# Six attention layers on one core: the odd heads' softmax exponentials move to ScalarE, head by head out of PSUM

## The reference

```python
q = l2norm(q) * qs ; k = l2norm(k) * ksc
q = q * cos * scale + rotate_half(q) * sin * scale
k = k * cos / scale + rotate_half(k) * sin / scale
sim = einsum('bhwie,bhwje->bhwij', bq, bk2) * 8.0
sim = where(mask, -max, sim)
attn = softmax(sim, -1)
out = einsum('bhwij,bhwje->bhwie', attn, bv2)
```

## Time and profile before

| | |
|---|---|
| median of 3 runs | 1926.08 us (1924.15 to 1927.91) |
| the profiled execution | span 1924.9 us; the page gives no other time of it |
| PE busy | 1751.1 us, 91% of the span |
| PEld busy | 1185.3 us, 62% |
| DVE busy | 1550.0 us, 81% |
| ACT busy | 1138.0 us, 59% |
| POOL busy | 1259.8 us, 65% |
| mean granted TensorE clock | 0.958 of full |
| chain that ended last | PE 40%, DVE 22%, issue 11%, POOL 9%, DMA 7%, ACT 4% |

### The profile page before, as it was taken

How to read it: one execution, slowest core, us unless ns; L and a number is a source line. 1 busy time by engine, 2 the same in 40 slices (tenths; PEclk the granted TensorE clock), 3 DMA queues, 4 the chain that set the end, 5 groups by cost and what they waited for, 6 DMA issues and landing times.

```text
span 1924.9 us, 72907 instructions
## 1 busy us (share of the span) xinstructions
PE 1751.1 (91%) x31158; PEld 1185.3 (62%) x31158; DVE 1550.0 (81%) x2150; ACT 1138.0 (59%) x2221; POOL 1259.8 (65%) x981
## 2 busy tenths in 40 slices
PE   7577876899999989999899999899998999999985
PEld 2144553466666666667666767666666676666663
DVE  6599957788888878888888888788887888888853
ACT  5523223557676747676667676667675667676742
POOL 3476743777777767777667777677776777777730
PEclk9699977999999989999999999999998999999986
DMA  4534201222222232222322222322223222222220
GB/s 97 127 53 51 29 3 70 58 67 70 69 73 68 72 104 79 63 75 70 112 66 79 69 73 83 103 62 77 69 72 109 69 68 79 63 76 67 70 61 26
DMA packets 68257, 137.27 MB, mean 71 GB/s; under 512 B 17952, under 2 KB 23520, under 8 KB 66912
## 3 DMA queue, kind: packets, MB, share of 16 engines
q1 hardware_dynamic: 67936, 132.62, 27.0%
HBM read 29.79 MB, written 2.10 MB: 17 GB/s over the span
## 4 chain that ended last, share of the span: by engine, by line
PE 40%; DVE 22%; issue 11%; POOL 9%; DMA 7%; ACT 4%; SPq 2%; DVEq 0%; ACTq 0%; POOLq 0%
PE bank L1460 9%; PE bank L1370 6%; PE bank L1443 6%; POOL rot L1308 5%; DMA v_shift<-v_tok 5%; DVE rot L1770 5%; PE bank L1418 5%; PE bank L1501 3%; PE bank L1375 3%; PE bank L1477 3%; DVE total L1796 2%; DVE rnorm L1776 2%; POOL probs L1332 2%; DVE probs L1789 2%; DMA p_T<-p_blocks 1%
## 5 line engine op out<-in xcount | busy, mean ns | idle before, releaser
L1770 DVE TENSOR_TENSOR rot<-bank,gains 128x1024 f32<-128x1024 f32 x384 | 462.3, 1206 | 158.8 <-ACT squares L1603 142.8
L1314 POOL TENSOR_TENSOR rot<-rot,rnorm 128x1024 f32<-128x1024 f32 x192 | 361.0, 1901 | 319.3 <-ACT rnorm L1613 317.1
L1308 POOL TENSOR_TENSOR rot<-rot 128x512 f32<-128x512 f32 x384 | 480.6, 1274 | 6.9 <-DVE rot L1770 6.9
L1370 PE MATMUL bank<-wqkv,x 128*128 128x512 f32 x768 | 404.9, 612 | 10.5 <-issue 5.0
L1603 ACT ACTIVATE squares<-bank 128x512 f32<-128x512 f32 x384 | 232.8, 606 | 256.5 <-PE bank L1370 255.9
L1332 POOL TENSOR_TENSOR probs<-probs,total 128x1024 f32<-128x1024 f32 x96 | 182.7, 1903 | 125.3 <-DVE total L1798 125.3
L1644 ACT ACTIVATE o_T<-bank 128x512 f32<-128x512 f32 x192 | 104.2, 598 | 254.2 <-PE bank L1443 254.2
L1776 DVE TENSOR_REDUCE rnorm<-squares 128x16 f32<-128x1024 f32 x192 | 233.0, 1214 | 2.8
L1443 PE MATMUL bank<-p_T,v_shift 64*64 64x32 f32 x6144 | 194.7, 223 | 26.6 <-DMA p_T<-p_blocks 21.9
L1443 PEld LDWEIGHTS bank<-p_T,v_shift 64*64 64x64 f32 x6144 | 169.2, 138 | 79.1 <-issue 49.6
L1383 PEld LDWEIGHTS bank<-st_ident,rot 128*128 128x128 f32 x1536 | 179.9, 143 | 59.9 <-issue 53.6
(11 more groups left out here) (196 smaller groups left out, 2849.2 us busy)
## 6 DMA issues: line engine op xcount, KB each, us to landing
p_T<-p_blocks SPq DMA_DIRECT2D x768, 64.0 KB
v_shift<-v_tok SPq DMA_DIRECT2D x96, 384.0 KB, 3.5
v_shift<-v_tok SPq DMA_DIRECT2D x96, 128.0 KB, 3.4
wqkv<-in_wqkv SPq DMA_DIRECT2D x6, 1536.0 KB, 8.0
v_rep_sb<-v_by_step SPq DMA_DIRECT2D x32, 128.0 KB
v_rep<-v_by_step SPq DMA_DIRECT2D x32, 128.0 KB
wo<-in_wo SPq DMA_DIRECT2D x6, 512.0 KB, 8.6
w<-in_w SPq DMA_DIRECT2D x6, 341.0 KB, 8.8
```

The source lines that it names most:

```text
L1308: nc.gpsimd.tensor_tensor(out=out, in0=out, in1=by_head(turned[:, part])[:, :, frm], op=ALU.add).then_inc(rot_added.sem, 1)
L1314: nc.gpsimd.tensor_tensor(out=by_head(qk[u][:, half]), in0=by_head(qk[u][:, half]), in1=rnorm[u][:, AH * i:AH * (i + 1)].unsqueeze(2).to_b ...
L1370: nc.tensor.matmul(QK_BANKS[i][:, :], shifted_tokens(x, n, P), layer_cols(wqkv, n, 3 * INNER, 512 * i, 512), start=True, stop=True).then_i ...
L1770: nc.vector.tensor_tensor(both, src.unsqueeze(1).to_broadcast([P, 2, 8, DH]), pair_of_gains.unsqueeze(2).to_broadcast([P, 2, 8, DH]), ALU. ...
```

## The change

`shifts` and `totals` handle the even heads only (bank 4). The odd heads' exponentials are taken by ACT straight from bank 5, one head at a time: eight activations of 64 columns, each with the head's negated peak as its per-row bias, and each writing the head's sum as a second result into `total`. The even heads keep one exponential, now over 8 x 64 columns. The factor 8 moves from the activation into the query's rotary tables on the host. `peaks` does the odd heads first, and negates them. `exp_made` counts two per block, the first after the odd heads. PE's wait in `outputs` is now for `shifted` (bank 4 read by DVE) and for `exp_made(.., 1)` (bank 5 read by ACT).

```diff
-    s_product, peak_made, shifted, exp_made = sig("s_product"), sig("peak_made", per=2), sig("shifted", per=2), sig("exp_made")
+    s_product, peak_made, shifted, exp_made = sig("s_product"), sig("peak_made", per=2), sig("shifted"), sig("exp_made", per=2)
...
             else:
+                pe.wait_ge(exp_made.sem, exp_made.after(n - 1, 1))
                 transposes(S_BANKS, q_turned, qk[n % 2][:, 0:INNER], oT_made, n - 2)
...
                 if n < LAST - 1:
                     pe.wait_ge(shifted.sem, shifted.after(n + 1))
+                    pe.wait_ge(exp_made.sem, exp_made.after(n + 1, 1))
...
         def exponent(n):
+            u = n % 2
+            act.wait_ge(peak_made.sem, peak_made.after(n, 1))
+            act.wait_ge(p_turned.sem, p_turned.after(n - 2))
+            act.wait_ge(p_normed.sem, p_normed.after(n - 2))
+            for a_ in range(PAIRS):
+                head = nc.scalar.activation(probs[u][:, a_, 1, :], s_banks(n)[1][:, 2 * WINDOW * a_:2 * WINDOW * (a_ + 1)], ACT.Exp,
+                                            bias=peak[u][:, 1, a_:a_ + 1], accum_out=total[u][:, 2 * a_ + 1:2 * a_ + 2])
+            head.then_inc(exp_made.sem, 1)
             act.wait_ge(shifted.sem, shifted.after(n))
-            pr = probs[n % 2][:, :, :, :].rearrange("p a b d -> p (a b d)")
-            nc.scalar.activation(pr, pr, ACT.Exp, scale=QK_SCALE).then_inc(exp_made.sem, 1)
+            pr = probs[u][:, :, 0, :]
+            nc.scalar.activation(pr, pr, ACT.Exp).then_inc(exp_made.sem, 1)
...
-            for p in range(2):
+            dve.wait_ge(exp_made.sem, exp_made.after(n - 2, 1))
+            for p in (1, 0):
                 s = s_banks(n)[p][:, :].rearrange("p (a k) -> p a k", a=PAIRS)
-                nc.vector.reduce_max(peak[n % 2][:, p, :], s, AX).then_inc(peak_made.sem, 1)
+                nc.vector.tensor_reduce(peak[n % 2][:, p, :], s, AX, ALU.max, negate=(p == 1)).then_inc(peak_made.sem, 1)
...
-            for p in range(2):
-                s = s_banks(n)[p][:, :].rearrange("p (a k) -> p a k", a=PAIRS)
-                dve.wait_ge(peak_made.sem, peak_made.after(n, p + 1))
-                nc.vector.tensor_tensor(probs[n % 2][:, :, p, :], s, peak[n % 2][:, p, :].unsqueeze(2).to_broadcast([P, PAIRS, DH]),
-                                        ALU.subtract).then_inc(shifted.sem, 1)
+            dve.wait_ge(peak_made.sem, peak_made.after(n))
+            s = s_banks(n)[0][:, :].rearrange("p (a k) -> p a k", a=PAIRS)
+            nc.vector.tensor_tensor(probs[n % 2][:, :, 0, :], s, peak[n % 2][:, 0, :].unsqueeze(2).to_broadcast([P, PAIRS, DH]),
+                                    ALU.subtract).then_inc(shifted.sem, 1)
...
-            nc.vector.reduce_sum(total[u][:, :], probs[u][:, :, :, :].rearrange("p a b d -> p (a b) d"), AX).then_inc(total_made.sem, 1)
+            nc.vector.reduce_sum(total[u][:, :].rearrange("p (a b) -> p b a", b=2)[:, 0, :], probs[u][:, :, 0, :], AX).then_inc(total_made.sem, 1)
...
-    for s in (scale, f(1.0) / scale):
+    for s in (f(QK_SCALE) * scale, f(1.0) / scale):
```

More of the change, by code:

```diff
@@ L1432, in outputs @@
                     pe.wait_ge(shifted.sem, shifted.after(n))
+                    pe.wait_ge(exp_made.sem, exp_made.after(n, 1))
                 pe.wait_ge(v_read.sem, v_read.after(n))
```

## The result

The changed kernel takes 2162.13 us (median of 4 runs, 2155.72 to 2164.53) against 1925.12 us for the kernel before on the same chip: a ratio of 1.123 [1.1205, 1.1256] (in brackets the 95% interval, here and below). It is slower by 237 us. The forecast was 2067 us, slower by 141, and its range ended at 2135. The profiled execution of the changed kernel has a span of 2162.6 us.

A forecast was written before the change was run, and what follows sets the result against it. The prediction took PE to be the bound. It added 42 gate turns x (2.3 us wait + 1.0 us clock loss) = 139 us and about 2 us at the program's end to 1926, giving 2067 us; range 1985 to 2135.

The forecast's parts named there:

- The head step: ACT's time per odd head, bias and second result included: 0.28 us, with bounds of 0.18 and 0.38.
- The wait: PE's stall at `outputs` for ACT to finish bank 5: 2.3 us, in 42 gate turns.
- DVE's busy time: Expected in the changed kernel's profile: DVE busy down by about 116 us, ACT up by about 190.
- the clock: Behind three of five gate-turn stalls PE loses 1.7 us at 1.2 GHz: 1.0 us a gate turn, bounds none and all.
- The stretches of the earlier trace: Two PE idle stretches: after 3.25 us the clock fell, costing 1.7 us; after 1.84 us it stayed at 2.4 GHz.
- The output turn: nothing: In output turns `project_o` covers ACT's reading of bank 5 with 1.2 us left, so the cost is nothing.
- DVE's relief: Shorter `shifts` and `totals` save DVE 1.21 us in each of 96 blocks, landing in idle time: worth 0.
- ACT's nine instructions: In gate turns they make ACT's later work 1.8 us later, but PE is 2.3 us later: nothing added to PE's delay.
- The rival with DVE as the bound: PE has hidden slack, so 96 x 1.21 us of DVE come off: 1810 us; chance 0.03 for faster.
- the rule of the Trainium skill: Weight-load busy time, not matmul busy time, shows PE's nearness to its limit; DVE at 81 to 85% is more contended.

The follow-up runs named there:

- e1: Kernel before with DVE's shifts and sums cut to the even heads, ACT keeping its single exponential over 1024 columns; 1918.53 us, 0.9957.
- e7: Kernel before with PE waiting in `outputs` for the next block's one exponential instead of its shifts; 1958.48 us, 1.0165.
- e6: Changed kernel without the second result: eight activations with a bias alone, all sums on DVE again; 2072.51 us, 1.0766.
- e3: Changed kernel with four copies and one exponential of 512 columns replacing ACT's sixteen short instructions, DVE summing all heads; 2184.35 us, 1.1346.
- e12: Changed kernel with PE waiting in `outputs` for the even heads' exponential too; 2153.79 us, 1.1174.
- e10: Changed kernel with PE's spare waits taken out, leaving as many waits on PE as before; 2161.0 us, 1.1201.
- e9: Kernel before with two added waits on PE that are always satisfied; 1927.32 us, 1.0003.
- e11: e4 with PE's spare waits taken out; 1972.9 us, 1.0241.
- e4: Changed kernel with the odd heads' eight exponentials moved ahead of square 2 and square 3 on ACT; 1970.62 us, 1.0228.
- e5: The change in the output turns' (odd) blocks only, the kernel before in the other blocks; 1946.42 us, 1.0105.
- e2: Kernel before with ACT's nine instructions taking shifted scores from SBUF, PE waiting for the shifts only; 2037.84 us, 1.0579.

## Why the prediction missed

**Right, by its steps.** PE was the bound (e1). The head step was forecast at 0.28 us and measured 0.29. The wait was forecast at 2.3 us in some 42 gate turns and measured 2.31 in 43 turns (99.1 us), with none in the output turns. DVE's busy time fell by 91 us (forecast 116) and ACT's rose by 201 (forecast 190). Of the 231.8 us in the 45 pairs, this wait is about 92: 99.1 less the 6.9 us by which the DMA waits for `p_T` shrank. The forecast had 97.

**The step that failed is the clock:** "I take it that three of five stalls are followed by such a piece: 0.6 x 1.7 = 1.0 us a gate turn", 42 us in all. The granted clock cost 106 us more than before, 94 of them in PE's busy time: 2.2 us a gate turn where the forecast had 1.0, and more than its upper bound of 1.7. Both of its factors were too small. Of the 43 waits, 38 (not three in five) are followed by time at 1.2 GHz before the next wait: 12 of them by a loss of about 1.7 us, as in the windows above, and 26 by 3.0 to 5.1 us, mostly 3.4. The mean of the 38 is 3.0 us where the forecast had 1.7. The stretches of the earlier trace rows are one of each outcome, and two single cases give neither a share nor a size.

The runs give the price in place. With a wait of 0.84 us (e7) the clock costs nothing. With 1.56 us (e6) it costs 44 us over 43 gate turns, with 2.31 us (the change) 106, with 2.38 us (e3) 90, with 2.77 us (e12) 89 in the profiled execution and some 20 and 30 more in the two others. These sums hold the stretches inside `outputs` as well. Without them, in gate turns where the wait is the only idle stretch over 0.4 us, the clock fell after none of 28 waits of 0.84 us and after 3 of 12 of 1.56 us (1.7 us each). It fell after all 10 of 2.31 us (2.4 us on average; in e10 after all 12) and, in e12, by 1.7 us or more after 21 of 31 of 2.77 us. So a wait of 2.3 us is enough by itself, and most of e6's 44 us follow other stretches.

**A term that was missing:** the stretches inside `outputs`, 28 us more than before, and 12 us more of other unexplained idle time, most of it at the first matmuls of the scores. With the 92 of the wait and 5 us of waits for `xm` these make the 138 us of idle time. PE's timeline shows such a stretch:

```profile
822.43 0.32 PE L1446 MATMUL bank<-p_T,v_shift 64*64 64x32 f32 x8 [2.31 <-issue]
...
823.70 0.33 PE L1446 MATMUL bank<-p_T,v_tok 64*64 64x32 f32 x8
826.30 0.44 PE L1446 MATMUL bank<-p_T,v_shift 64*64 64x32 f32 x8 [2.27 <-issue]
```

The DMA view of 822 to 828 us, in 40 slices of 0.15 us, has a packet of the queue that carries instructions in the slice at 823.8, just as PE falls idle; PE goes on at 826.30, 2.4 us later:

```profile
DMA  0000000000003000000000000000000000000040
...
q8 instruction: 2, 0.03, 2.1%
```

One case is only a suspicion, but the traces of all 14 kernels hold more. Each has 217 packets of 16,384 bytes on that queue in its 45 pairs. Every one of the 161 stretches inside `outputs`, in whatever kernel, ends 2.2 to 3.0 us after the start of such a packet, and those at the first matmuls of the scores do so too (2.2 to 3.2 us). A moment taken at random has a packet start that far behind it in 12 to 14% of cases, and none of the 41 waits at the start of `outputs` that the profile calls issue has one. So in these stretches PE very likely stands still until its next instructions are there. Not every packet stops PE: one starts at 827.7, and PE goes on.

What is left is why the change has more of such stretches from as many packets. The packets start at other points of PE's program: 77 of the 90 runs of `outputs` have one start inside them in the change, 44 in the kernel before. What the runs exclude as the cause of that is the number of ScalarE's instructions (e3), the added waits as instructions (e9, e10, e11), and PE's wait as such (e7 has one stretch and e12 none, though both wait; e4 has the stretches and no wait). Why the fetches come late stays open. It concerns 28 of the 237 us, 12 more at the scores, and part of the clock cost behind them.

**Smaller terms.** "The output turn: nothing" was right for the wait at `outputs`, but e5 shows 20 us for the whole of the change there. DVE's relief, put at 0, is worth 8 us (e1). ACT's nine instructions, put at nothing, are hidden behind the wait here; without it a queue of that kind cost 110 us (e2). The rival with DVE as the bound (1810 us) falls with e1. So does, for this kernel, the rule of the Trainium skill behind it ("Perfetto Trace Analysis", Identifying the Most-Contended Engine): PE's weight loads were at 62% and DVE at 81%, and still 90 us less of DVE gave 8.

No variant that moves the odd heads to ACT beats the kernel before. The nearest that do all the work are e5 (1.011) and e4 (1.023), and e1 shows that DVE's relief had at most 0.4% to give.

## What to carry to other kernels

Before work is moved to a less busy engine, look at where it will stand in that engine's queue and who needs its input buffer next. Here an engine at 59% read the bank at the one point at which the bounding engine wanted it back, and 2.3 us of wait in every second turn cost twice that. Price a recurring wait of the matmul engine by a run with a wait of that length in that place. Here 0.84 us cost its own length and 2.3 us cost about 4.5. When a saved wait or a freed engine is the reason for a change, first run the relief alone (e1 here): its 0.4% would have settled the matter.

## What the hardware showed that was not expected

- An activation's second result is a separate `ACTIVATION_READ_ACCUMULATOR` (record 0.227 us) that adds 0.09 us to the step between heads: 0.29 us with it, 0.195 without (e6), 64 columns from PSUM with a bias. In e2, from SBUF and in place, the step with it was 0.33 us.
- The clock cost depends on how the idle time is laid out. e2 adds 79 us of idle time in pieces of up to 1.3 us and loses no clock; the change adds 138 us, mostly in pieces of 2.3 us, and loses 106 us.
- A longer wait left the total where it was: 2.77 us instead of 2.31 (e12) removed every idle stretch inside `outputs`, 31 us in the pairs, for 20 us more of waiting, while the clock cost varied from run to run (182 to 215 us of the whole program).
- PE's idle stretches inside `outputs` go with the fetching of instructions: all 161 in the 14 kernels, up to 2.4 us long, end 2.2 to 3.0 us after a packet of 16,384 bytes starts on the queue that carries instructions.
